# L0 and the RNN's input product two tiles ahead of the RNN instead of one, in a fused four-layer sequence kernel

## What is computed

```python
ys = cond / sqrt(512);  d = rsqrt((ys*ys) @ (w0*w0) + 1e-8)
x1 = x + ((x * ys) @ w0) * d                      # L0
h_t = tanh(h_{t-1} @ wh1 + x1_t @ wx1 + b1)       # L1, h_{-1} = cond
x2 = x1 + h
A, B = gelu(layernorm(cond) @ w1 + b1') @ w2 + b2 # per sequence, 512 x 8 each
x3 = 2*x2 + x2 @ (base + A @ B^T)                 # L2
gates_t = x3_t @ wx3 + h_{t-1} @ wh3 + b3         # L3, an LSTM, 4 x 512 gates
out = x3 + h
```

## Time and profile before

| | us |
|---|---|
| median of 3 runs (lowest, highest) | 1172.07 (1172.05, 1172.1) |
| the profiled execution: its own time | 1172.2 |
| its span in the trace | 1170.4 |
| PE busy in the span | 1129.6 (97%) |
| DVE busy | 895.7 (77%) |
| ACT busy | 424.4 (36%) |
| POOL busy | 53.9 (5%) |
| mean granted clock of PE | 0.995 |

### The profile page before, as it was taken

The page is one execution under the profiler, slowest core; times in us unless marked ns, Lnnn a source line. Parts: engine busy times, 40 slices in busy tenths (PEclk is TensorE's granted clock), DMA queues, the critical chain, the costliest instruction groups (busy, mean ns, idle before and its releaser), DMA issues.

```text
span 1170.4 us, 52110 instructions
## 1 busy us (share of the span) xinstructions
PE 1129.6 (97%) x23548; PEld 773.6 (66%) x23548; DVE 895.7 (77%) x2656; ACT 424.4 (36%) x1036; POOL 53.9 (5%) x75
## 2 busy tenths in 40 slices
PE   5779999999999999999999999999999999999997
PEld 3446766776676677667766766776676677667587
DVE  6798777777877777787777777777777777777665
ACT  6784333333333333333333332333333233333322
POOL 1000100000000000000000000000000000000000
PEclk9899999999999999999999999999999999999999
DMA  9991000000000000000000000000000000000000
GB/s 337 404 348 29 21 21 21 3 21 21 21 20 21 21 3 21 21 21 21 20 21 3 21 20 21 21 21 21 3 21 21 21 21 21 11 5 10 11 13 21
DMA packets 24590, 51.08 MB, mean 44 GB/s; under 512 B 4160, under 2 KB 4288, under 8 KB 23344
## 3 DMA queue, kind: packets, MB, share of 16 engines
q1 hardware_dynamic: 24080, 47.56, 11.4%
q10 hardware_dynamic: 288, 0.20, 0.1%
HBM read 39.36 MB, written 8.39 MB: 41 GB/s over the span
## 4 chain that ended last, share of the span: by engine, by line
PE 92%; DMA 4%; SPq 2%; DVE 2%; ACT 1%; issue 0%; DVEq 0%; ACTq 0%
PE ps_gates L1463 55%; PE ps_l L1399 14%; PE ps_x L1399 7%; PE ps_rnn L1509 6%; PE ps_rnn L1512 4%; DMA ring<-in_hw 2%; PE ps_lr L1399 2%; PE ps_z L1399 2%; PE ps_l L1463 1%; DMA big<-in_hw 1%; SPq L394 1%; PE ps_gates L1369 1%; SPq L426 1%; DVE gates_ring L1074 0%; ACT rows L514 0%
## 5 line engine op out<-in xcount | busy, mean ns | idle before, releaser
L1463 PE MATMUL ps_gates<-big,lstm_h 128*32 128x512 f16 (+1 forms) x6144 | 344.7, 373 | 2.0 <-DVE lstm_h L1106 2.0
L1463 PE MATMUL ps_gates<-big,rows 128*32 128x512 f16 (+1 forms) x6144 | 342.9, 372 | 0.6 <-ACT rows L514 0.6
L1463 PEld LDWEIGHTS ps_gates<-big,rows 128*32 128x32 f16 x6144 | 165.6, 97 | 157.7 <-issue 1.2
L1463 PEld LDWEIGHTS ps_gates<-big,lstm_h 128*32 128x32 f16 x6144 | 157.8, 97 | 150.1 <-DVE lstm_h L1106 3.4
L650 ACT ACTIVATE gates_ring<-gates_ring 128x256 f32<-128x256 f32 x128 | 53.4, 417 | 339.6 <-DVE gates_ring L1074 339.6
L1074 DVE SCALAR_TENSOR_TENSOR gates_ring<-ps_gates,tile_un,rows 128x256 f32<-128x256 f32 x248 | 108.7, 478 | 75.2 <-PE ps_gates L1463 72.8
L1509 PE MATMUL ps_rnn<-rnn_h,wh_hi 128*128 128x64 f16 x2048 | 120.5, 192 | 4.8 <-DVE rnn_h L908 4.8
L1509 PEld LDWEIGHTS ps_rnn<-rnn_h,wh_hi 128*128 128x128 f16 x2048 | 93.0, 97 | 37.0 <-issue 27.1
L1512 PE MATMUL ps_rnn<-rnn_h,wh_lo 128*128 128x32 f16 x2048 | 116.3, 177 | 0.0
L1103 DVE SCALAR_TENSOR_TENSOR late<-gates_ring,tile_g,cell_tanh 128x128 f16<-128x128 f32 x128 | 45.0, 351 | 60.7 <-ACT cell_tanh L659 60.7
L1512 PEld LDWEIGHTS ps_rnn<-rnn_h,wh_lo 128*128 128x128 f16 x2048 | 91.1, 97 | 0.0
(11 more groups left out here) (199 smaller groups left out, 1597.2 us busy)
## 6 DMA issues: line engine op xcount, KB each, us to landing
ring<-in_hw SPq DMA_DIRECT2D x16, 1024.0 KB, 14.7
xT_sb<-in_xT SPq DMA_DIRECT2D x32, 256.0 KB, 2.9
outT<-late SPq DMA_DIRECT2D x32, 256.0 KB, 2.0
big<-in_wx SPq DMA_DIRECT2D x5, 1024.0 KB, 14.0
big<-in_wh SPq DMA_DIRECT2D x5, 1024.0 KB, 15.5
big<-in_w SPq DMA_DIRECT2D x1, 1024.0 KB, 7.9
big<-in_hw SPq DMA_DIRECT2D x1, 1024.0 KB, 13.5
late<-in_base SPq DMA_DIRECT2D x1, 1024.0 KB, 14.4
```

The lines of the kernel that those rows point to most:

```text
L1463: last = nc.tensor.matmul(by_chunk_of_gate(bank[B * j:B * j + B, columns]), of_step, tile_columns(w, j)[:, gates], start=start, stop=stop, ...
```

## The change

L0 and L1's input product run two tiles ahead of the RNN (`LEAD = 2`): iteration i has them for tile i+2, so the loop's last such tile is reached one iteration earlier, and the loading has four tiles of them instead of three. x1 gets 3 buffers, xw1 2 and x2 3. The fourth xw1 of the loading is done in the first iteration. Tile 4's magnitude, its reduce on POOL and its scales are done in the loading. SP issues x tile 4 ahead of the b3 loads. The orders of ACT, DVE and PE in the first half of the loading are laid anew; their second half stays, with the tile numbers raised by one. DVE's layernorm waits for cond's rows alone, and for the gain and bias rows (semaphore `ld_ln`) only later. ACT takes the layernorm's root ahead of w0's squares. The diff, cut to its core, in the order SP, POOL, ACT, DVE, PE; index changes of the rings (`c % 2` to `c % X1_RING`, `x2_ready` counts, `l0_scaled` in `move_b`) are left out.

```diff
-X2_RING = 5
+X2_RING = 3
+LEAD = 2
+X1_RING = 3
...
-        x1T = [sb(f"x1T{q}", [P, KC, STEPS, B]) for q in range(2)]
-        xw1T = sb("xw1T", [P, KC, STEPS, B])
+        x1T = [sb(f"x1T{q}", [P, KC, STEPS, B]) for q in range(X1_RING)]
+        xw1T = [sb(f"xw1T{q}", [P, KC, STEPS, B]) for q in range(LEAD)]
...
         def in_l0(i):
-            return i + 1 < TILES
+            return i + LEAD < TILES
...
+            sp.wait_ge(x1_ready, 1)
+            load_x(XT_RING)
             sp.wait_ge(a_ps, 2)
             sp.wait_ge(a_max_ready, 1)
             for j in range(KC):
                 for g in range(GATES):
                     sp.dma_start(by_gate(b3_sb[B * j:B * j + B])[:, g],
...
-            sp.wait_ge(x1_ready, 1)
-            load_x(XT_RING)
+            sp.wait_ge(x1_ready, 2)
+            load_x(XT_RING + 1)
             for i in range(LAG, TILES + LAG):
-                a, c = i - LAG, i + XT_RING - 1
+                a, c = i - LAG, i + XT_RING
                 if c < TILES:
-                    sp.wait_ge(x1_ready, i)
+                    sp.wait_ge(x1_ready, i + 1)
                     load_x(c)
...
             spread(slice(16, 19))
+            pool.wait_ge(m_ready, LAG + LEAD + 1)
+            pool.wait_ge(tile_s_ready, LAG + LEAD)
+            spread_x(0, 1)
             pool.wait_ge(wh3_lo_ready, 2 * KC)
-            xs(LAG + 1)
-            for i in range(LAG, TILES - 2):
-                pool.wait_ge(m_ready, i + 3)
-                pool.wait_ge(tile_s_ready, i + 2)
+            xs(LAG + LEAD)
+            for i in range(LAG, TILES - LEAD - 1):
+                pool.wait_ge(m_ready, i + LEAD + 2)
+                pool.wait_ge(tile_s_ready, i + LEAD + 1)
                 spread_x(0, 1)
-                xs(i + 2)
+                xs(i + LEAD + 1)
...
             act.dma_start(ln_rows[:, 0], cond).then_inc(ld_rows, 16)
-            act.dma_start(ln_rows[:, 1], ln_g.partition_broadcast(B)).then_inc(ld_rows, 16)
-            act.dma_start(ln_rows[:, 2], ln_b.partition_broadcast(B)).then_inc(ld_rows, 16)
+            act.dma_start(ln_rows[:, 1], ln_g.partition_broadcast(B)).then_inc(ld_ln, 16)
+            act.dma_start(ln_rows[:, 2], ln_b.partition_broadcast(B)).then_inc(ld_ln, 16)
...
             x1_high(0)
+            copy_rows(0)
+            xs_high(1)
             wx3_squares(0)
-            xs_high(1)
+            xs_high(2)
+            rnn(0)
             wx3_squares(1)
             wx3_squares(2)
             wx3_squares(3)
-            copy_rows(0)
             x1_high(1)
-            rnn(0)
             wx3_high(0, 0)
+            rnn(1)
             wx3_high(0, 1)
             wx3_high(1, 0)
-            rnn(1)
+            x1_high(2)
             wx3_high(1, 1)
-            xs_high(2)
+            xs_high(3)
             wx3_high(2, 0)
             wx3_high(2, 1)
             copy_rows(1)
...
-                a1, c, t, r = i - LAG + 1, i + 1, STEPS * (i - LAG), STEPS * i
+                a1, c, t, r = i - LAG + 1, i + LEAD, STEPS * (i - LAG), STEPS * i
...
-            dve.wait_ge(ld_rows, 48)
+            dve.wait_ge(ld_rows, 16)
...
             over_power(scales[:, 7:8], exps[:, 7:8], TOP).then_inc(h_scale_ready, 1)
+            x_magnitude(0, 0)
+            xs(0)
+            dve.wait_ge(ld_ln, 32)
+            linked(nc.vector.tensor_tensor(ae, ae, ln_rows[:, 1], ALU.mult))
+            nc.vector.tensor_tensor(ae, ae, ln_rows[:, 2], ALU.add).then_inc(ae_ready, 1)
             weight_scale(1, 2, w0_scale_ready)
...
             x1(0)
-            wh1_low(0)
+            for oc in range(KC - 1):
+                wh1_low(oc)
+            x1_low(0)
             x_magnitude(1, 1)
             xs(1)
             x_magnitude(2, 2)
             x_magnitude(3, 3)
-            x1_low(0)
+            wh1_low(KC - 1)
             tile_scales(1, XT_RING - 1, 1)
-            wh1_low(1)
+            tile_undo(1, XT_RING - 1, 1)
             xs_low(1)
-            wh1_low(2)
             xs(2)
-            wh1_low(3)
             dve.wait_ge(ld_b1, 16)
             xw1(0)
-            tile_undo(1, XT_RING - 1, 1)
+            rnn_sums(0)
+            xs_low(2)
             x1(1)
-            rnn_sums(0)
+            xs(3)
+            rnn_out(0)
+            x1(2)
+            rnn_sums(1)
             wx3_scale()
             x1_low(1)
-            rnn_out(0)
             wx3_low(0, 0)
-            rnn_sums(1)
+            rnn_out(1)
             wx3_low(0, 1)
-            rnn_out(1)
+            xw1(1)
             wx3_low(1, 0)
+            x1_low(2)
             wx3_low(1, 1)
             rnn_sums(2)
+            wx3_low(2, 0)
             base_diagonal()
-            wx3_low(2, 0)
             rnn_out(2)
             a_magnitude()
-            xs_low(2)
+            xs_low(3)
             rnn_sums(3)
...
             x2(0)
-            xw1(1)
+            xw1(2)
             rnn_sums(4)
-            x1(2)
+            x1(3)
...
             gate_scales(0)
+            x_magnitude(LAG + LEAD, 0)
             x3_first(0)
...
             x2_low(1)
+            tile_scales(LAG + LEAD, 1, 0)
+            tile_undo(LAG + LEAD, 1, 0)
             gate_scales(1)
-            xw1(2)
...
                 rnn_out(r + 1)
                 if i == LAG:
-                    x_magnitude(LAG + 2, 0)
+                    xw1(LAG + 1)
+                    x_magnitude(LAG + LEAD + 1, 0)
...
             l1(0)
-            l0(1)
             pe.wait_ge(wh1_lo_ready, KC)
             pe.wait_ge(h0_lo, 1)
             rnn(0)
+            l0(1)
+            l0(2)
+            rnn(1)
             w2_unit(4)
-            rnn(1)
+            l1(1)
+            rnn(2)
             w2_unit(5)
             w2_unit(6)
-            rnn(2)
             w2_unit(7)
-            l1(1)
+            l1(2)
             turn_a()
             rnn(3)
-            l0(2)
+            l0(3)
             rnn(4)
             w2_unit(8)
```

More of the change, by code:

```diff
@@ L15 @@
 BH = B // 2
-FB = P // KC
 ZN = STEPS * BH
@@ L672, in _ @@
             nc.scalar.activation(unused[:], cell[:, 0:1], ACT.Sqrt)
+            act.wait_ge(ln_var_ready, 1)
+            nc.scalar.activation(ln_s[:, 1:2], ln_s[:, 0:1], ACT.Sqrt).then_inc(ln_root_ready, 1)
             act.wait_ge(ld_w0, 16)
             squares(big[:, SQ_SLOT], big[:, W0_SLOT], 1)
-            act.wait_ge(ln_var_ready, 1)
-            nc.scalar.activation(ln_s[:, 1:2], ln_s[:, 0:1], ACT.Sqrt).then_inc(ln_root_ready, 1)
             act.wait_ge(ld_wx1, 16)
@@ L728, in _ @@
             base_high(0)
-            x1_high(2)
+            x1_high(3)
             wh3_squares(1)
@@ L755, in _ @@
             x2_high(1)
-            xs_high(LAG + 1)
+            xs_high(LAG + LEAD)
             for i in range(LAG, TILES):
-                a1, c, t, r = i - LAG + 1, i + 1, STEPS * (i - LAG), STEPS * i
+                a1, c, t, r = i - LAG + 1, i + LEAD, STEPS * (i - LAG), STEPS * i
                 lstm_acts(t)
@@ L872, in x1 @@
                 linked(nc.vector.tensor_scalar(d_un[:], dT[:], tile_s[:, c, 3:4], None, ALU.mult))
-                wait(dve, x2_ready, c - 1)
+                wait(dve, x2_ready, c - X1_RING + 1)
                 dve.wait_ge(l0_ps, c + 1)
-                nc.vector.tensor_tensor(x1T[c % 2][:], ps_l0[:].rearrange("p (k t b) -> p k t b", t=STEPS, b=B),
+                nc.vector.tensor_tensor(x1T[c % X1_RING][:], ps_l0[:].rearrange("p (k t b) -> p k t b", t=STEPS, b=B),
                                         d_un[:].unsqueeze(2).broadcast_to([P, KC, STEPS, B]), ALU.mult)\
@@ L878, in x1 @@
                 dve.wait_ge(l0_scaled, c + 1)
-                nc.vector.tensor_tensor(x1T[c % 2][:], x1T[c % 2][:], xT_sb[c % XT_RING][:], ALU.add).then_inc(x1_ready, 1)
+                nc.vector.tensor_tensor(x1T[c % X1_RING][:], x1T[c % X1_RING][:], xT_sb[c % XT_RING][:], ALU.add).then_inc(x1_ready, 1)
             def x1_low(c):
                 dve.wait_ge(x1_hi_ready, c + 1)
-                low(x1_16[:, 1], x1T[c % 2][:].rearrange("p k t b -> p k (t b)"), tile_s[:, c, 1:2], x1_16[:, 0])\
+                low(x1_16[:, 1], x1T[c % X1_RING][:].rearrange("p k t b -> p k (t b)"), tile_s[:, c, 1:2], x1_16[:, 0])\
                     .then_inc(x1_lo_ready, 1)
@@ L898, in rnn_sums @@
                 sums = ps_rnn[:, 0:2 * P].rearrange("p (k h b) -> p k h b", h=2, b=B)
-                nc.vector.scalar_tensor_tensor(rnn_half[:], sums[:, :, 1], un_rnn[:], xw1T[:, :, s],
+                nc.vector.scalar_tensor_tensor(rnn_half[:], sums[:, :, 1], un_rnn[:], xw1T[i % LEAD][:, :, s],
                                                ALU.mult, ALU.add).then_inc(rnn_half_ready, 1)
@@ L1236, in _ @@
             wx3_low(2, 1)
-            x1_low(2)
+            x1_low(3)
             wx3_low(3, 0)
@@ L1270, in _ @@
             x2_low(1)
+            tile_scales(LAG + LEAD, 1, 0)
+            tile_undo(LAG + LEAD, 1, 0)
             gate_scales(1)
-            xw1(2)
             dve.wait_ge(ld_b3, 16 * KC * GATES)
```

(7 more changed lines are left out.)

28 lines of the change are left out of this document (11 added, 17 removed).

## The result

The changed kernel takes 1175.85 us (median of 8 runs, 1174.30 to 1176.39) against 1172.06 for the kernel before (8 runs beside it, 1171.94 to 1173.88): a ratio of the means of 1.0029, 95% interval 1.0018 to 1.0040. The kernel is slower. The interval begins just under the 0.2% up to which the prediction speaks of no change.

A forecast was written before the change was run, and what follows sets the result against it. The loading ends with w2 loads and DVE together; then PE runs without waits until the last iteration. Loop end -2.1, loading +2.65, clock +0.9 and first iteration +0.2 sum to +1.65, forecasting 1173.7 us, range 1170.1 to 1176.2.

The forecast's parts named there:

- signs of being right: Listed trace observations, from loading to loop end, that would confirm the forecast, such as the last wx3 square ending near 47.3 us.
- signs of being wrong: Squares done by 44, first gate product before 95.5, late DMA wait at units 14 or 15, or mid-loop PE waits.
- Loop end, -2.1: Iteration 30 without L0 and L1: each half 1.07 us shorter, PE still waiting for rnn_h; -2.1 us.
- The scales of tiles 1 to 3, +2.0: Early loading on DVE: the scales of tiles 1 to 3 end at 35.7 us, formerly 33.7.
- ACT is where time is lost: Loading: wx3 squares wait behind xs_high(1) and xs_high(2), ending at 47.3 instead of 43.2; rnn_out(3) 3.6 us late.
- Some 0.35 of the lag goes where rnn_sums(5) waits for PE now, and the 0.60 before the maximum goes: Loading after rnn_out(3): these idle times reduce the 3.6 us lag to +2.65 us at the last maximum.
- The first iteration, +0.2: Tile 4's reduce on POOL delays xs(4), and xw1(3) precedes lstm_sums(9); +0.2 us, bounds 0 and 0.9.
- hidden loading: Rival: the added tile fits in the loading's idle time, leaving 0 to 1 us of lag; 1170.5 us, chance 0.23.
- slow clock: Rival: all of l0(2) at half clock, 2.68 us, and the lag undiminished through busy DVE; 1175.5 us, chance 0.19.
- packed iteration: Rival: iteration 30 has no stall and all 5.4 us come back; 1170.4, or 1167 if loading hides; chance 0.08.
- The clock at the start: First 10 us: PE idle yet granted clock 1.00, unlike the half-rate default that activity releases.

The follow-up runs named there:

- e_split: Changed kernel; in iterations 30 and 31 a third (16 matmuls) of a gates' input product moved ahead of each half's second RNN step; 1172.52 us.
- e_undo: Changed kernel with the old order of its first 15 us restored on DVE and ACT; 1176.03 us.
- e_fill2: Changed kernel with 36 dead matmuls on PE ahead of rnn(5) and as many ahead of rnn(6); 1175.12 us.
- e_allfill: Changed kernel with the edits of e_act2, e_split and e_fill2, and tile 4's magnitude moved ahead of b's scale; 1170.89 us.
- e_act2: Changed kernel with wx3 square 0 ahead of xs_high(1), squares 1 and 2 ahead of xs_high(2) on ACT, wx3 scale ahead of x1(2) on DVE; 1174.40 us.

## Why the forecast was 2.2 us too low

The forecast was no change (0.57, against 0.35 for slower) and the kernel is slower. Of its signs of being right, the waits at the loop's end, the squares (47.8), rnn_out(3) (65.90) and the low clock after 42.8 are there; the last maximum (92.40, for 90.3 to 91.5) and the first gate product (99.31, for 97 to 98.5) came later than stated. Its signs of being wrong did not appear. The steps in turn:

- **Loop end, -2.1:** measured -2.14 (two halves of 15.95 against 17.02), and e_split shows the cause. What the step left out is the tail: PE's two waits for `lstm_h` grew from 2.0 to 2.3 in total. With it the stretch gives -1.8.
- **The scales of tiles 1 to 3, +2.0:** measured +2.1. The order was walked correctly, and e_undo shows no cost of the start. That the two agree to 0.1 us is luck, since the scales of the variants lay 1.6 us apart.
- **"ACT is where time is lost" and the clock, +3.6 and +0.9 at rnn_out(3), 4.5 in all:** measured 5.2 (65.90 against 60.72). The squares ended at 47.8 for 47.3. The clock fell over l0(2) as forecast, from 44 on, and made it 1.5 us longer, of which at most 1.1 counted at the wx3 scale, for 0.9. Without it the squares would have come last, as the prediction has it; with it x1(2) did. The missing 0.7 us is all there at the first wx3_high already (50.61 for 49.0 + 0.9): from there to rnn_out(3) it took 15.29 us for 15.35 walked. The mechanism held, and both sizes were somewhat too small.
- **"Some 0.35 of the lag goes where rnn_sums(5) waits for PE now, and the 0.60 before the maximum goes":** this step failed. 0.38 came back, not 0.95. The 0.60 did go, but two low stretches of the clock that were not in the forecast (71 to 75 and 78 to 82 us) gave DVE a new wait of 0.48 on PE. With the clock held up the stretch took 25.80 us instead of 26.50 in both executions (e_fill2, e_allfill), which would have been 1.1 given back.
- **The first iteration, +0.2:** the term that was mis-sized most, +1.0 (bounds 0 to 0.9). The working had the lstm's need met to within 0.1 us of 116.8, and then forgot l0(4), which needs xs_low(4) and came 0.23 late. POOL's gap was 7.60 for the 7.05 taken. The Trainium skill (GPSIMD Engine Reference, 2.1 Instruction dispatch) has about 6 us for a first call of freshly loaded code; an estimate by it would make the gap here 1.6 shorter. The trace has 7.60, and the trace decides; no run here shows whether this gap is such a loading.
- **The rivals:** the hidden loading did not occur. The slow clock had l0(2) longer by 2.68 us (1.8 above the forecast's 0.9), for 1.5 measured. Its other half, that the lag goes undiminished through the busy DVE, held nearly, but through later low stretches that it didn't name. That its 1175.5 is within 0.4 us is partly luck, for 0.8 us of the miss is the first iteration's, which it doesn't have. The packed iteration did not occur, the four waits are there.
- **The clock at the start:** the prediction says that the granted clock is 1.00 in the first 10 us. The column does show 1.00 from 0 to 33 us, but the matmul records there don't agree with it: in the kernel before, the first 8 matmuls of l0(0) take 1.04 us, as such 8 do where the column shows 0.50 (1.01 to 1.06 us in e_allfill's l0(2)), against 0.62 for the same in l0(1) at 37.21. So the prediction's "not in the first 10 us" rests on a column that doesn't show the clock there.

```profile
22.22 1.04 PE L1399 MATMUL ps_l<-xs,w_hi 128*128 128x128 f16 x8
```

- Sum: -2.1 + 4.8 + 1.0 + 0.3 = 4.0 us.

Open: in which executions the clock falls ahead of l0(1), and so how much of the 3.8 us between the medians it holds; and how much of the 3.1 us that the stretch up to rnn_out(3) is longer could be won, of which e_act2 got 0.9. A kernel with fillers at all four idle times was not run, nor one in which e_act2's order has work of DVE cut, which would show both limits of the first half at once.
